# Retention layer with an int8 gate: row sums moved between ScalarE and VectorE, in the row statistics and in the head epilogue

## What is computed

```python
xn = layernorm(x)                                   # row mean and row variance over 1024
q, k = xn @ wq, (xn @ wk) * 128 ** -0.5             # 8 heads of 128; rotated by sin/cos
v, g = xn @ wv, xn @ wg                             # 8 heads of 256
qk = (qr @ kr.T) * mask                             # lower triangle with a decay per head
qk = qk / clip(abs(qk.sum(-1)), 1)
out = qk @ v
out = out * rsqrt(mean(out * out, -1) + 1e-5)       # over the 256 columns of the head
s = (silu(g) * out) @ wo
gate = silu(int8_matmul(xn, rhs))                   # rows of xn scaled by their absolute maximum
y = x + s * gate
```

## Time and profile before

| | us |
|---|---|
| median of three runs | 1457.27 |
| the three runs | 1455.26, 1457.27, 1534.32 |
| the profiled execution | 1457.36 |
| its span on the slowest core, first to last instruction | 1455.6 |
| spans of its eight cores | 1436.1 to 1455.6 |
| busy: TensorE matmul | 854.7 |
| busy: VectorE | 680.8 |
| busy: ScalarE | 384.2 |
| busy: GpSimd | 89.0 |

### The profile page before, as it was taken

How to read it: one execution, slowest core, us unless ns; L and a number is a source line. 1 busy time by engine, 2 the same in 40 slices (tenths; PEclk the granted TensorE clock), 3 DMA queues, 4 the chain that set the end, 5 groups by cost and what they waited for, 6 DMA issues and landing times.

```text
span 1455.6 us, 15469 instructions; the slowest of 8 cores (1436.1 to 1455.6 us)
## 1 busy us (share of the span) xinstructions
PE 854.7 (59%) x4720; PEld 486.5 (33%) x4768; DVE 680.8 (47%) x1509; ACT 384.2 (26%) x646; POOL 89.0 (6%) x105
## 2 busy tenths in 40 slices
PE   0111675875865654485449544844585557788776
PEld 0000533723723532272127122612452323233232
DVE  1444135135356855676566657666755421111211
ACT  0443323313323211241233032312331311111211
POOL 1000001001000001000100010001000101111121
PEclk9999996975995885588559655975696558889888
DMA  7411005005116105100500050015001431121121
GB/s 119 102 58 58 16 1 73 1 0 73 59 38 109 29 15 72 44 17 28 87 15 30 15 87 15 30 22 80 16 29 15 59 43 58 58 87 58 58 67 64
DMA packets 52657, 69.32 MB, mean 48 GB/s; under 512 B 19424, under 2 KB 35936, under 8 KB 52576
## 3 DMA queue, kind: packets, MB, share of 16 engines
q0 software_dynamic: 38608, 26.32, 13.6%
q1 hardware_dynamic: 13968, 42.01, 9.1%
HBM read 86.25 MB, written 8.39 MB: 65 GB/s over the span
## 4 chain that ended last, share of the span: by engine, by line
PE 45%; DVE 26%; issue 14%; ACT 12%; DMA 2%; DVEq 1%; ACTq 0%; POOL 0%; SPq 0%; POOLq 0%
PE psG L1075 10%; DVE arena L560 6%; PE psX L765 4%; PE psB L765 4%; PE psX L738 4%; DVE arena L556 4%; PE psB L738 3%; PE psX L712 3%; PE psB L712 2%; PE psG L885 2%; ACT arena L773 2%; PE psA L1097 2%; DVE arena L866 2%; PE psB L1097 2%; PE psX L776 2%
## 5 line engine op out<-in xcount | busy, mean ns | idle before, releaser
L885 PE MATMUL psG<-arena 128*128 128x257 bf16 x320 | 84.8, 391 | 161.8 <-ACT arena L871 155.2
L1075 PE MATMUL psG<-arena 128*128 128x512 bf16 x496 | 144.4, 457 | 54.0 <-DVE arena L1119 52.0
L560 DVE TENSOR_TENSOR arena<-arena 128x1024 f16<-128x1024 f16 x192 | 132.9, 692 | 20.4 <-DVE arena L556 0.5
L783 DVE TENSOR_TENSOR arena<-arena 128x512 bf16<-128x512 bf16 x64 | 27.2, 425 | 189.7 <-ACT arena L773 189.7
L885 PEld LDWEIGHTS psG<-arena 128*128 128x128 bf16 x320 | 33.1, 120 | 214.4 <-issue 206.7
L1075 PEld LDWEIGHTS psG<-arena 128*128 128x128 bf16 x512 | 57.0, 114 | 141.2 <-issue 103.8
L1107 DVE TENSOR_TENSOR arena<-psA,arena 128x512 f32<-128x512 f32 x16 | 11.1, 692 | 194.2 <-PE psA L1097 194.2
L477 PE MATMUL psT<-arena 128*128 128x128 bf16 x128 | 16.2, 305 | 144.4 <-DVE arena L471 129.0
L765 PE MATMUL psX<-arena 128*128 128x512 bf16 x248 | 77.1, 466 | 27.7 <-DVE arena L786 27.3
L556 DVE TENSOR_SCALAR arena<-arena 128x1024 f16<-128x1024 f16 x192 | 82.1, 428 | 21.4 <-DVE arena L560 1.4
L776 PE MATMUL psX<-arena 128*128 128x512 bf16 x64 | 27.6, 431 | 96.2 <-ACT arena L773 54.2
(11 more groups left out here) (125 smaller groups left out, 1372.2 us busy)
## 6 DMA issues: line engine op xcount, KB each, us to landing
arena<-x_tm SPq DMA_DIRECT2D x48, 512.0 KB, 3.6
arena<-rhsT SPq DMA_DIRECT2D x16, 512.0 KB, 3.5
out<-arena SPq DMA_DIRECT2D x32, 256.0 KB, 2.2
arena<-wv POOLq DMA_DIRECT2D x8, 512.0 KB, 8.0
arena<-wg POOLq DMA_DIRECT2D x8, 512.0 KB, 6.2
arena<-aba POOLq DMA_DIRECT2D x8, 512.0 KB, 8.0
arena<-abb POOLq DMA_DIRECT2D x8, 512.0 KB, 5.3
arena<-wo POOLq DMA_DIRECT2D x16, 256.0 KB, 3.8
```

Of the source, the lines that this page charges most:

```text
L560: p.op(V, (lambda bsrc=bsrc, th=th: lambda v: v.tensor_add(bwh[:, 0:1024], bsrc[:, 0:1024], th[:, 0:1024]))(), reads=bx + ([buf_] if first ...
L885: gI=gI, rJ=rJ: lambda t: t.matmul(ps_g[:, 512 * ii:512 * ii + 257], scsb[:, sso + 128 * ii:sso + 128 * ii + 128], vr[:, VRS * Jt:VRS * Jt ...
L1075: ins = t.matmul(ps_g[:, go + 512 * hf:go + 512 * hf + 512], ztens[:, zc:zc + 128], wo_b[:, 1024 * c + 512 * hf:1024 * c + 512 * hf + 512] ...
```

## The change

In stage 0, the sum of a row and the sum of its squares are no longer taken by ScalarE's accumulator. ScalarE only squares the tile into `ep`; VectorE sums the tile itself (a third reduction) and then sums `ep` (a fourth). `Identity` is gone, and the ScalarE instruction no longer writes `b_stc`.

In the epilogue, piece 1 is no longer a VectorE product and a VectorE reduction but four ScalarE `Square` instructions of 128 by 256, each with `accum_out` into a column of `ecb`. They read `epb` and write both the scratch tile `zsb` and `ecb`.

```diff
-            p.op(SC, (lambda sl=sl, i=i: lambda s: s.activation(
-                ep[:, 0:1024], sl, AF.Square,
-                accum_out=stc[:, 16 + i:17 + i]))(),
-                reads=bsl, writes=[b_ep, b_stc])
-            p.op(SC, (lambda sl=sl, i=i: lambda s: s.activation(
-                ep[:, 0:1024], sl, AF.Identity,
-                accum_out=stc[:, i:i + 1]))(),
-                reads=bsl, writes=[b_ep, b_stc])
+            p.op(V, (lambda sl=sl, i=i: lambda v: v.reduce_sum(
+                stc[:, i:i + 1], sl, axis=AX.X))(),
+                reads=bsl, writes=[b_stc])
+            p.op(SC, (lambda sl=sl: lambda s: s.activation(
+                ep[:, 0:1024], sl, AF.Square))(),
+                reads=bsl, writes=[b_ep])
+            p.op(V, (lambda i=i: lambda v: v.reduce_sum(
+                stc[:, 16 + i:17 + i], ep[:, 0:1024], axis=AX.X))(),
+                reads=[b_ep], writes=[b_stc])
...
-                pieces.append(lambda: (
-                    p.op(V, lambda v: v.tensor_mul(zsb[:, :], epb[:, :],
-                                                   epb[:, :]),
-                         reads=epw, writes=zsw),
-                    p.op(V, lambda v: v.tensor_reduce(
-                        ecb[:, 8:12],
-                        zsb[:, :].rearrange("p (i s) -> p i s", i=4),
-                        axis=AX.X, op=ALU.add),
-                        reads=zsw, writes=ecw)))
+                def sspiece():
+                    for ii in range(4):
+                        p.op(SC, (lambda ii=ii: lambda s: s.activation(
+                            zsb[:, 256 * ii:256 * ii + 256],
+                            epb[:, 256 * ii:256 * ii + 256], AF.Square,
+                            accum_out=ecb[:, 8 + ii:9 + ii]))(),
+                            reads=epw, writes=zsw + ecw)
+                pieces.append(sspiece)
```

## The result

| | before | after |
|---|---|---|
| median over 10 runs, slowest core | 1457.4 us | 1481.44 us |
| ratio, with its 95% interval | 1 | 1.0171 [1.0143, 1.020] |
| profiled execution | 1457.36 | 1481.48 |
| its span on the slowest core | 1455.6 | 1479.6 |
| spans of its eight cores | 1436.1 to 1455.6 | 1448.1 to 1479.6 |

A forecast was written before the change was run, and what follows sets the result against it. The prediction took the kernel to be bound by engines waiting for one another, no engine being full. It summed 1457.36 + 0.3 (stage 0) + 15.7 (epilogues) + 1.1 (head starts) = 1474.5 us, range 1462 to 1487.

The forecast's parts named there:

- What bounds the kernel: Whole kernel: engines waiting for one another bound it, so an edit costs what it adds to such chains.
- the two chains: Stage 0's serial VectorE and ScalarE tile chain, 5.12 us a tile, and the epilogue's stretch 927 to 939, 2.19 us.
- Stage 0: Stage 0: a tile goes from 5.12 to 5.28 us; first group -1.1, three others +1.4, together +0.3 us.
- The epilogue: Lines 927 to 939: +0.49 us in each of 32 epilogues, 15.7 us, plus 1.1 us at four head starts.
- The sum: Whole kernel: 1457.36 + 0.3 + 15.7 + 1.1 = 1474.5 us, 1.2% slower.
- rival 3: Head starts: one more TensorE stretch at 1.2 GHz at each of eight heads, 14.8 us, 1489 us; chance 9%.
- Masks decide: Inner steps: line 866's mask sets the pace and runs earlier, -19 us, 1438 us; chance 3%.
- One more table load: Heads, ScalarE: the set loaded for `Sqrt` lacks `Square`, one more load a head, 10.3 us, 1484.8 us; chance 8%.
- Nothing moves: Epilogues: the added half microsecond falls where another engine is later anyway, 1457 to 1462 us; chance 8%.

The follow-up runs named there:

- e3_delay: Kernel before plus two small VectorE instructions in front of line 939 in each epilogue, nothing moved to ScalarE; 1479.45 us against 1458.69, ratio 1.014.
- e4_double: Changed kernel with each of an epilogue's four squares issued twice; 1565.57 us, ratio 1.072 to the kernel before.
- e8_nowait: Changed kernel with the squares' sums in a tile and buffer names of their own; 1456.36 us, ratio 0.997 to the kernel before.
- e5_split: Kernel before with the epilogue's squares shared, two blocks on ScalarE, two on VectorE, sums and buffers of their own; 1426.66 us, ratio 0.978.

## Why the prediction was right, and what was off

**What bounds the kernel.** Right, and the largest use of it: the two chains read from the timeline were priced by their waits, not by busy time, and e3_delay and e4_double moved the mean core by slightly more than what they added to the chain (20.9 us for 17.9, 86.7 for 78.6), with no engine's busy time deciding.

**Stage 0.** A tile is 5.29 us, 5.28 was forecast; the table load runs beside the first maximum; up to the first `Silu` load it came out +0.6 in the mean core where +0.3 was forecast. Part of that is the first tile's arrival, 0.3 us earlier in this execution; from the first maximum to the heads' first matmul it is 134.2 us against 133.0, +1.2, within the 2 us that the forecast allowed. As a statement on the stage it held. As a statement on the kernel with this edit alone it missed 6 to 8 us at a lower clock, which neither this step nor a rival named.

**The epilogue.** The pitch of the squares (0.60), the hand-over from the reciprocal (0.27 to 0.28), the length of the stretch (2.68 to 2.69) and the time of a square (0.416 us against 0.415 worked out from 4 and 1024 elements) all came as reckoned:

```profile
L932 ACT ACTIVATE arena<-arena 128x256 bf16<-128x256 bf16 x128 | 53.3, 416 | 26.0 <-DVE arena L928 16.8 <-DVE arena L867 0.4
...
L932 ACT ACTIVATION_READ_ACCUMULATOR arena<-arena 128x1 f32 x128 | 23.8, 186 | 0.0
```

Five epilogues, not four, had their squares held up by a ScalarE copy, by 0.26 us each. Together 15.7 + 1.1 = 16.8 was forecast, 17.0 measured.

**The sum.** 17.1 was forecast, 24 measured on the slowest core, 20.3 in the mean core. At equal clock the change is +12.4 us (1463.5 against 1451.1, both at 0.79), which is below the forecast, since over the 32 stretches the granted clock is 0.59 before and 0.64 after, far below the core's mean: making them longer lowers the mean clock by itself. Of the mean core's 20.3 us the stretches hold 17.0 and stage 0 about 1, so some 2 to 3 are left; another 2 lie in the greater distance of the slowest core from the mean core, 13.2 instead of 11.0; and the last 1 to 2 are within what the kernel before differs by from series to series. The term that was mis-sized is the clock. I had it as rival 3, all or nothing, with a stretch at 1.2 GHz more at each head's start, 14.8 us and 9%. That did not come: in the first 3.7 us of the projections at seven head starts and on eight cores the granted clock was 0.54 in the mean before the change and 0.62 after it. What came is uneven between cores and lies, in the profiled execution, in the projections of q and k; that the 2 to 3 us of the mean core are clock too is read from the fitted line and not shown instruction by instruction. Costing it at nothing in the main sum was the mistake; the spans of the eight cores of the kernel before, 1436.1 to 1455.6 with clocks from 0.799 to 0.779, had already shown that the clock makes 20 us here.

**Rivals.** Masks decide: no; the mask did run early, at 241.06, and nothing came of it, for the copy behind it waited for the squares until 242.33, as the rival's condition said. One more table load: no. The load groups on ScalarE are as before, one each ahead of `Silu` and ahead of `Sqrt`, so `Square` runs under both sets:

```profile
L747 ACT ACT_TABLE_LOAD x8 | 10.3, 1283 | 6.7 <-PE psX L739 6.7
L952 ACT ACT_TABLE_LOAD x8 | 10.3, 1283 | 7.3 <-DVE arena L949 7.3
...
L461 ACT ACT_TABLE_LOAD x1 | 1.3, 1283 | 27.5 <-DMA arena<-x_tm 27.5
```

Nothing moves: no.

**What the forecast did not see** is that most of the price came from names of buffers and not from the work. I took the wait for the reciprocal as given and priced it at 0.27 us. e8_nowait shows that the wait for each other of instructions that merely share the 16-column tile `ecb`, in both directions together, is worth all of the change's cost. The Trainium skill, "VectorE: DVE Perf Modes", "Rules for kernel authors", advises to restructure a reduction away from a hot path. The edit did so and lost, since the path waited for the sum whichever engine made it; e5_split, which brings the time to the sum from 2.19 us to 1.39, is the restructuring that pays. The kernel before with names of their own and nothing moved was not run.

## What to carry to other kernels

Moving work to an idle engine helps only if the result arrives earlier: write down the stretch from the instruction that releases the work to the one that needs it, on both engines, hand-overs included, and multiply that difference. Before moving anything, look for instructions that wait for each other only because they write columns of one named buffer; giving each engine's results a name of their own was worth 35 us in stage 0, and here all that the move had cost. With several cores, compare the mean core and the granted clock beside the slowest, and put the spread of the cores into the range.

## What the runs showed of the hardware

- A core's span follows its mean granted TensorE clock at -1.1 us per 0.001, with 2.6 us scatter, and the mean clock of a core of one and the same program lies between 0.767 and 0.804 from run to run. The median of the slowest core stands 8 to 17 us above the mean core, by kernel, 12 for the kernel before and 15 for the changed one.
- An edit that leaves the heads' instructions alone and makes stage 0 about 1 us longer changed the mean clock by -0.006 and -0.009 in its two series; together with another epilogue (e8_nowait) it did not. Why is open.
- TensorE's waits of 0.8 to 1.0 us between groups of eight matmuls come with either level of the clock: a group of 128x512 takes 1.89 us at 2.4 GHz, and up to 3.6 where the clock is at 1.2.
- A `Square` with an accumulator costs 0.60 us for 256 columns, of which 0.19 is the read of the accumulator and 0.20 the fixed part of an ACTIVATE, worked out from 205 ns at 4 elements and 1057 at 1024; from the first of four on 1024 columns to the start of line 939 it took 2.41 us, where product and reduction on VectorE took 2.09 (from 623.34 to 625.43 in the fifth head's start before the change).
